# Two load buffers for the half blocks of w1, and a later place for two low parts of h

## The reference

```
x = x + tanh(g_xattn[0]) * attention(layernorm(x), ctx)            # 8 heads of 64, 750 keys
logits = layernorm(x) @ gate_w.T + gate_b ; gates = softmax(rmsnorm(logits) / 0.5) ; g = top 1
h = gelu(xf @ w1[e] + b1[e])  for all 8 experts e   (512 -> 1024)
y = h @ w2[e] + b2[e]                                (1024 -> 512)
x = x + tanh(g_ffn[0]) * sum over e of y * g/(g + 1e-6)
```

## Time and profile before

| | |
|---|---|
| three runs | 1829.84, 1837.42 (median), 1839.65 us |
| the profiled execution | 1831.34 us, its span 1829.6 us |
| PE busy | 1772.1 us (97%), granted clock 0.997 |
| DVE, POOL, ACT busy | 1470.2 (80%), 1364.4 (75%), 942.4 us (52%) |
| chain that ended last | 69% on PE, 8% DVE, 5% DMA, 5% POOL |

### The profile page before, as it was taken

One profiled execution on the slowest core, in us unless ns is written; L12 is line 12 of the kernel. 1 busy time (PEld: TensorE's weight loads), 2 busy tenths in 40 slices (PEclk: granted clock), 3 DMA queues, 4 the chain that ended last, 5 costly groups with the idle time before them and its releaser, 6 DMA issues.

```text
span 1829.6 us, 35734 instructions
## 1 busy us (share of the span) xinstructions
PE 1772.1 (97%) x9780; PEld 1621.6 (89%) x9780; DVE 1470.2 (80%) x2532; ACT 942.4 (52%) x1832; POOL 1364.4 (75%) x1334
## 2 busy tenths in 40 slices
PE   7899999999999999999999999999999999999998
PEld 7799999999999978888888888888899999999997
DVE  6688878888878875876777678768989989989987
ACT  6576676766667754434343434334444444444443
POOL 5667676766767668777677767767989889889873
PEclk9899999999999999999999999999999999999999
DMA  5233434243351345334433433354433433433422
GB/s 175 79 101 96 117 86 134 69 109 99 95 142 50 103 141 220 127 120 172 155 126 125 171 151 126 141 187 162 161 132 132 151 126 133 154 123 135 154 104 92
DMA packets 120065, 236.78 MB, mean 129 GB/s; under 512 B 14392, under 2 KB 91192, under 8 KB 111808
## 3 DMA queue, kind: packets, MB, share of 16 engines
q1 hardware_dynamic: 120000, 235.99, 38.5%
HBM read 166.24 MB, written 69.73 MB: 129 GB/s over the span
## 4 chain that ended last, share of the span: by engine, by line
PE 69%; issue 9%; DVE 8%; DMA 5%; POOL 5%; ACT 2%; SPq 2%; DVEq 0%; POOLq 0%; ACTq 0%
PE scores L1004 26%; PE bank L1074 16%; PE bank L1045 10%; PE bank L861 8%; DMA w_stage<-in_L_ffn_w 3%; PE bank L942 3%; DVE acc_t L1478 2%; PE scores L932 2%; PE bank L954 2%; DMA xa<-in_x 1%; POOL w2s L2007 1%; POOL probs L1917 1%; DVE h_sum L1407 1%; SPq L720 1%; POOL w2s L2005 1%
## 5 line engine op out<-in xcount | busy, mean ns | idle before, releaser
L1004 PE MATMUL scores<-xs,w1s 128*128 128x448 f32 x2646 | 577.1, 367 | 3.1 <-ACT h_sum L1654 2.4
L1004 PEld LDWEIGHTS scores<-xs,w1s 128*128 128x128 f32 x2646 | 494.4, 188 | 52.0 <-ACT h_sum L1654 8.7
L1478 DVE TENSOR_TENSOR acc_t<-bank,acc_t 128x448 f32<-128x448 f32 x608 | 350.1, 614 | 18.8 <-PE bank L1074 18.7
L1654 ACT ACTIVATE h_sum<-scores 128x448 f32<-128x448 f32 x189 | 101.9, 539 | 238.3 <-PE scores L1004 238.2
L1407 DVE TENSOR_TENSOR h_sum<-scores,h_sum 128x448 f32<-128x448 f32 x189 | 117.0, 619 | 115.7 <-ACT h_sum L1654 55.6
L2145 POOL TENSOR_TENSOR hs<-h_full,hs 128x448 fp32r<-128x448 f32 x132 | 155.3, 1177 | 56.0 <-ACT hs L1813 55.1
L1045 PE MATMUL bank<-w2s,hs 128*128 128x512 f32 x798 | 189.5, 391 | 1.0 <-DVE xres L1367 1.0
L1045 PEld LDWEIGHTS bank<-w2s,hs 128*128 128x128 f32 x798 | 149.1, 188 | 31.2 <-issue 1.5
L1812 ACT ACTIVATE h_full<-h_sum,b1T 128x448 f32<-128x448 f32 x149 | 99.3, 667 | 129.9 <-DVE h_sum L1407 104.2
L1917 POOL TENSOR_SCALAR probs<-probs,row_inv 112x750 f32<-112x750 f32 x60 | 130.9, 2181 | 42.4 <-DVE row_inv L1338 42.1
L861 PE MATMUL bank<-ctxT,wk 128*128 128x376 f32 (+1 forms) x768 | 148.2, 342 | 8.9 <-DVE ctxT L1249 8.9
(11 more groups left out here) (178 smaller groups left out, 3718.9 us busy)
## 6 DMA issues: line engine op xcount, KB each, us to landing
w1s<-w_scratch SPq DMA_DIRECT2D x46, 1792.0 KB, 7.4
w_stage<-in_L_ffn_w SPq DMA_DIRECT2D x82, 512.0 KB, 3.6
w_scratch<-w1s SPq DMA_DIRECT2D x18, 1792.0 KB, 6.1
w_scratch<-w2s SPq DMA_DIRECT2D x28, 896.0 KB, 5.3
w_stage<-in_L_ffn_w SPq DMA_DIRECT2D x28, 256.0 KB, 5.3
ctx_raw<-in_ctx SPq DMA_DIRECT2D x16, 376.0 KB, 3.2
ctx_raw<-in_ctx SPq DMA_DIRECT2D x14, 374.0 KB, 3.2
xa<-in_x SPq DMA_DIRECT2D x16, 224.0 KB, 4.3
```

What stands on the lines that cost most here:

```text
L1004: mm = pe.matmul(product_bank(g, name)[:, 0:TH], w1s[j % 2][:, s, W_OF[name], kc, :], xs[:, i, m, kc, :], start=opens and n == 0, stop=n == 5,
L1478: dve.tensor_tensor(home, bank, home, ALU.add).then_inc(z_added, 1)
L1654: return act.activation(dst, src, ACT.Copy, scale=scale)
```

## The change

In attention `split_ahead` reads its input from one of two load buffers, the old one for even k and a new tile `ahead_second` for odd k, each with its own semaphore; the sums stay in the second half of `w2_stage`. `load_ahead(b, k)` now waits for the split two places before it, and SP issues each load one place earlier: the load of E(k+1) stands where that of E(k) stood. POOL's split gets a wait for its own split before it. In the first batch `E1` moves on POOL from behind `E0` to behind `D1`. In the feed-forward stage the two low parts of h move on DVE from behind the additions k = 7 and 9 to behind k = 11 and 13.

```diff
+    early_pool = [i for i in FIRST["pool"] if i != ("E", 0, 1)]
+    d1 = early_pool.index(("D", 0, 1)) + 1
+    FIRST["pool"] = early_pool[:d1] + [("E", 0, 1)] + early_pool[d1:]
...
+            ahead_second = a("ahead_second", [P, 4, P])
...
-                if not (isinstance(b, int) and b == 0 and k == 0):
-                    sp.wait_ge(ahead_split, b * (2 * AHEAD) + 2 * k)
+                if not (isinstance(b, int) and b == 0 and k < 2):
+                    sp.wait_ge(ahead_split, b * (2 * AHEAD) + (2 * k - 2))
                     alone(sp, passed["sp"])
-                sp.dma_start(ahead_raw[:, 0:4, :], w1[e, j][:, :, c, :]).then_inc(ahead_loaded, 16)
+                sp.dma_start(ahead_in[k % 2], w1[e, j][:, :, c, :]).then_inc(ahead_loaded[k % 2], 16)
...
                 if name != "first":
                     store_ahead(b - 1, 2)
-                    load_ahead(b - 1, 3)
+                    if name != "last":
+                        load_ahead(b, 0)
                     store_ahead(b - 1, 3)
                 if name == "last":
                     load_w2((0, 0, 0))
                 else:
-                    load_ahead(b, 0)
+                    if name == "first":
+                        load_ahead(b, 0)
+                    load_ahead(b, 1)
...
                     store_ahead(b, 0)
-                    load_ahead(b, 1)
+                    load_ahead(b, 2)
...
                     store_ahead(b, 1)
-                    load_ahead(b, 2)
+                    load_ahead(b, 3)
...
                         elif row:
-                            if k in (7, 9):
-                                h_low(g, {7: 2, 9: 3}[k])
+                            if k in (11, 13):
+                                h_low(g, {11: 2, 13: 3}[k])
...
+                if not begin:
+                    pool.wait_ge(ahead_split, b * (2 * AHEAD) + 2 * k)
+                    alone(pool, passed["pool"])
-                pool.wait_ge(ahead_loaded, b * (16 * AHEAD) + 16 * (k + 1))
+                pool.wait_ge(ahead_loaded[k % 2], b * (8 * AHEAD) + 16 * (k // 2 + 1))
```

More of the change, by code:

```diff
@@ L307, in flamingo_kernel @@
             bo_t = a("bo_t", [P, D])
-        ahead_raw = w2_stage[:, :, :].rearrange("p a n -> p (a n)").rearrange("p (k n) -> p k n", k=8)
+            ahead_second = a("ahead_second", [P, 4, P])
+        ahead_first = w2_stage[:, :, :].rearrange("p a n -> p (a n)").rearrange("p (k n) -> p k n", k=8)
+        ahead_in = [ahead_first[:, 0:4, :], ahead_second[:, :, :]]
+        ahead_sums = ahead_first[:, 4:8, :]
         ahead_out = w2s[0][:, :, :, :].rearrange("p a b n -> p (a b n)")[:, 0:2 * NM * P].rearrange(
@@ L388, in flamingo_kernel @@
         w1_loaded, w1_step, w1_split = sem("w1_loaded"), sem("w1_step"), sem("w1_split")
-        ahead_loaded, ahead_step = sem("ahead_loaded"), sem("ahead_step")
+        ahead_loaded, ahead_step = [sem(f"ahead_loaded{i}") for i in range(2)], sem("ahead_step")
         ahead_split, ahead_stored = sem("ahead_split"), sem("ahead_stored")
@@ L1980, in split_ahead @@
             def split_ahead(b, k):
-                raw, w = ahead_raw, ahead_out
+                w = ahead_out
+                raw = [ahead_in[k % 2][:, i] for i in range(4)] + [ahead_sums[:, i] for i in range(4)]
+                given = ahead_in[k % 2][:, 1:4]
                 begin = isinstance(b, int) and b == 0 and k == 0
@@ L1987, in after @@
                     alone(pool, passed["pool"])
-                pool.wait_ge(ahead_loaded, b * (16 * AHEAD) + 16 * (k + 1))
+                if not begin:
+                    pool.wait_ge(ahead_split, b * (2 * AHEAD) + 2 * k)
+                    alone(pool, passed["pool"])
+                pool.wait_ge(ahead_loaded[k % 2], b * (8 * AHEAD) + 16 * (k // 2 + 1))
                 alone(pool, passed["pool"])
-                pool.tensor_tensor(raw[:, 4], raw[:, 0], raw[:, 3], ALU.add).then_inc(ahead_step, 1)
-                pool.tensor_tensor(raw[:, 6], raw[:, 1], raw[:, 0], ALU.subtract).then_inc(ahead_step, 1)
+                pool.tensor_tensor(raw[4], raw[0], raw[3], ALU.add).then_inc(ahead_step, 1)
+                pool.tensor_tensor(raw[6], raw[1], raw[0], ALU.subtract).then_inc(ahead_step, 1)
                 if not begin:
@@ L1995, in split_ahead @@
                     alone(pool, passed["pool"])
-                pool.tensor_copy(w[:, 0, 0:3], raw[:, 1:4]).then_inc(ahead_step, 1)
+                pool.tensor_copy(w[:, 0, 0:3], given).then_inc(ahead_step, 1)
                 after(1)
-                pool.tensor_tensor(raw[:, 5], raw[:, 4], raw[:, 1], ALU.subtract).then_inc(ahead_step, 1)
+                pool.tensor_tensor(raw[5], raw[4], raw[1], ALU.subtract).then_inc(ahead_step, 1)
                 after(3)
-                pool.tensor_tensor(w[:, 1, 0:3], raw[:, 1:4], w[:, 0, 0:3].bitcast(F32),
+                pool.tensor_tensor(w[:, 1, 0:3], given, w[:, 0, 0:3].bitcast(F32),
                                    ALU.subtract).then_inc(ahead_split, 1)
                 after(4)
-                pool.tensor_tensor(raw[:, 7], raw[:, 2], raw[:, 5], ALU.subtract).then_inc(ahead_step, 1)
+                pool.tensor_tensor(raw[7], raw[2], raw[5], ALU.subtract).then_inc(ahead_step, 1)
                 after(5)
-                pool.tensor_copy(w[:, 0, 3:7], raw[:, 4:8]).then_inc(ahead_step, 1)
+                pool.tensor_copy(w[:, 0, 3:7], ahead_sums[:, :, :]).then_inc(ahead_step, 1)
                 after(6)
-                pool.tensor_tensor(w[:, 1, 3:7], raw[:, 4:8], w[:, 0, 3:7].bitcast(F32),
+                pool.tensor_tensor(w[:, 1, 3:7], ahead_sums[:, :, :], w[:, 0, 3:7].bitcast(F32),
                                    ALU.subtract).then_inc(ahead_split, 1)
```

## The result

The changed kernel takes 1820.72 us (median of 5 runs, 1819.89 to 1821.67). The kernel before took 1835.82 us in 5 runs beside them (1829.84 to 1839.65). The ratio is 0.9921 [0.9899, 0.9943]: 14.5 us less. The forecast was 1813 in 1802 to 1826, so sign and range hold and the size is 7.7 us off.

The account below looks back on a forecast made before the run. PE is busy nearly throughout, so only removing its waits pays: 17.4 (lows) + 3.3 (middle batches) + 0.8 (first batch) = 21.5 us off 1831.34, 1809.8; half of 6.1 added gives 1813, range 1802 to 1826.

Parts of the forecast that it names:

- E1: POOL's split in attention: with the second load buffer it starts up to 1.59 us earlier in a middle batch.
- The lows of h: Feed-forward first half: moving both lows lets DVE add k = 8 before PE's P4 wants it; 17.4 us less over 13 steps.
- the rival on it: POOL operations go ahead of the second moved low, delaying the next sum: about 1834 (chance 0.02) or 1867 (0.03).
- the cover: Feed-forward row step: delay the sum, GELU and copy chain bears before PE waits; 0.53 us more, so the move costs nothing.
- The rival that P4 waits for something else: Feed-forward: DVE's additions are not what P4 waits for; only attention's 4.1 us come, 1827 to 1830; chance 0.06.
- The first batch: Attention's first batch: moving E1 frees T2.0, but the stall moves to T3.0 behind x's late rows; 0.8 us less.
- the slow stretch of the clock: First batch: the lower clock behind the stall comes once more behind the new stall, costing 1.9 us of the 2.7 gain.
- the rival at 1800 to 1804: First batch: the rows of x come in time, giving another 9.3 us; chance 0.09.
- The middle batches: Attention: the second load buffer starts E1 earlier, x's load moves up 0.55 us in each of six batches; 3.3 us less.
- E3: POOL's split in a middle batch: its rounding waits about 1 us for the store in place of the load's wait.
- The wait at T2.0: Middle batches: PE's 0.84 us wait for the probabilities POOL scales behind E1 was to go.
- the range of its own: Whole kernel: 1805 to 1822 us for the main forecast without rivals, from its terms' bounds and the 6 us to the median.

## Why the prediction was right, and where it was not

*The lows of h: right.* Forecast -17.4, measured -17.87 between the marks (1.37 for each of 13 steps) and -17.8 alone. The mechanism is the low that holds up the addition of k = 8: with only the low behind it moved, PE's wait stayed. The fear that POOL would hold the moved lows too (up to 2.8 us), and the rival on it, fell: 0.61 to 0.63 us. That the second low was not held at all was luck: it was forecast to meet POOL's long subtraction, a hold that the cover was to bear, and it started 0.09 us ahead of it (821.68 and 821.77). The rival that P4 waits for something else fell with the same rows.

*The first batch: right in its steps, and 0.8 us short.* E1 moved, T2.0 was free and the stall went on to T3.0. x's rows were forecast to land at 70.5 to 71.3 and were used at 70.72; T3.0 was forecast at 73.3 to 74.1 and came at 73.64. That both lie inside is in part luck, since the first P came 0.93 us earlier for no reason of the change. Counted from it, x's rows were used at 28.27 (forecast 27.1 to 27.9), and T3.0 gained 1.87 us (31.19 for 33.06; forecast 2.7, bounds 2.3 and 3.1). From T3.0 to the P of head 7 it lost 1.84 (42.60 for 40.76), and 1.9 was forecast for the slow stretch of the clock, which now stands behind T3.0. The rest is -0.03 for a forecast of -0.8. That the stall could be had away, the rival at 1800 to 1804, was shown by putting the load elsewhere, not by this change.

*The middle batches: wrong, in sign.* The step that failed: "With the second buffer the load is long there, so E1 starts up to 1.59 us earlier", followed by the 0.55 us for each batch from an `xa` (the second of the batch) that "was idle only 0.55 us for POOL's power". E1 did start earlier, and E3 does wait for the store in the load's place, as forecast (POOL's waits of after, 60 to 607 us: total us, times, longest):

```profile
POOL w2s L2011 <- DMA w_scratch<-w2s: 8.2, 7, 1.3
```

The wait at T2.0, of which the prediction says "that wait goes", stayed: 0.60 us in batches 2 to 6, where it was 0.65 to 0.84.

I asked only what stood behind E1 on POOL, not what ran beside it on DVE. POOL's 1.59 us of idle were the time in which DVE did its 0.54 us of `xa` undisturbed. With the gap gone, `xa` ran 2.64 us in five batches, and the keys behind it made PE wait. -3.3 became +4.9 (-1.31 + 6.2).

The Trainium skill, page "SBUF — State Buffer", section "SBUF: two separate sides", states the kind of collision: "the shared pair is an **exclusive lock**, not a bandwidth split". I weighed this rule for the lows, where the order turned out kind, and not for E1, which the second buffer brought onto `xa`. It lets the later one block until the other's instruction ends. Which of the page's conditions for such a lock `xa` meets, with one full-size input, no run here shows. The trace agrees that DVE stands still (2.64 us for 0.54) and goes further: `xa` waited not for one instruction of POOL but for a row of them, until POOL paused. The lows lost nothing because POOL paused in time.

What stays open: why batch 1 got away with 0.82 us. There too `xa` started 0.77 us behind E1's first operation, in every kernel with this order, and got in behind the first rounding.

*The size of the total.* Attention accounts for most of what is missing. The profiled pair gained 10.6 us of the 21.5: the middle batches are short by 8.2, the first by 0.8, and the other 1.9 are the sum of the stretches that gave what was forecast or were left alone. Timed alone, the two parts give -17.8 and +4.8 us, together -13.0 for the 14.5 measured. The base that I took, 1831.34 + 3, was sound: the three groups of runs of before have medians from 1831.42 to 1835.82. The upper end of the range of its own, 1822, does not follow from its terms: the least gain, 13.4 us, and the 6 us above the profiled execution give 1824. The result lies inside either.

## What to carry to other kernels

An idle gap of one engine may be the working time of another that shares something with it: before a wait on POOL is taken away, list what DVE does in that gap, and price it at the duration that the same shape has where POOL is busy. When a queue issues in program order, moving the consumer is half of the change: what stands behind its store in the queue moves too, and here reordering that queue was worth 7 to 10 us while the move alone was worth nothing. What needs no PSUM bank (here the lows of h) belongs behind the additions that free one: with the first low ahead of them PE lost 1.37 us a step, with both behind them nothing.

## What was unexpected of the hardware

A 0.54 us operation of DVE was held for 2.64 us by a row of POOL operations of 0.45 to 1.02 us each, and was let in only at POOL's pause of 0.17 us; the rows of batch 2 above show that it had been issued 0.77 us into that row.

In the last batch the granted clock fell to 0.50 in some executions and not in others, with almost the same work ahead of it. Busy time by stretch, of after (stretch, its length, PE, PEld, DVE, ACT, POOL, granted clock, DMA, GB/s):

```profile
640.00:650.00 10.00, 7.86 (x47) 5.77 (x45) 9.44 (x17) 9.68 (x20) 9.92 (x8) 1.00 0.09 26
652.00:656.00 4.00, 4.00 (x16) 3.77 (x16) 3.63 (x7) 3.41 (x7) 2.25 (x3) 0.50 0.41 59
```

and of before, at the same place in the batch, behind which the clock stayed at 1.00:

```profile
636.00:646.00 10.00, 7.97 (x47) 5.84 (x45) 9.38 (x17) 9.68 (x19) 9.92 (x8) 1.00 0.09 26
```

The last batch took 65.75 to 65.85 us in four profiles in which the clock stayed up and 66.60 to 67.21 in six in which it fell. Two of the six, with the attention of before and only lows moved, took 66.80 and 66.83 us, about 1 us more than before. So about 1 us of the +1.35 in the balance can be this, and not the change.
